# Cross-attention scores in tiles of 32 rows by 64 columns, with a PSUM bank for each row of tiles

## The reference, cut to what matters

```python
q = _ln((x @ Wq + bq).reshape(b, s1, H, HD), qn_w, qn_b)      # 16 heads of 32; 64 queries a batch
k = _ln(kv[..., :HD], kn_w, kn_b)                             # 1585 keys a batch, and 16 more of a second kind
def _attn(q, k, v):
    s = jnp.einsum('bhqd,bhkd->bhqk', q, k) * SCALE
    p = jax.nn.softmax(s, axis=-1)
    return jnp.einsum('bhqk,bhkd->bhqd', p, v)
```

## Time and profile before

| what | before |
|---|---|
| median of 3 runs | 1488.43 us |
| span of the profiled execution | 1487.2 us (1.2 below the median; the page gives no other time of this execution) |
| instructions | 41615 |
| PE busy | 1399.9 us, 94% |
| DVE, ACT, POOL busy | 860.5, 778.8, 500.8 us |
| cross-attention loop | from about 92 to 1182 us |

### The profile page before, as it was taken

The page is one execution under the profiler, slowest core; times in us unless marked ns, Lnnn a source line. Parts: engine busy times, 40 slices in busy tenths (PEclk is TensorE's granted clock), DMA queues, the critical chain, the costliest instruction groups (busy, mean ns, idle before and its releaser), DMA issues. The chain is left out here.

```text
span 1487.2 us, 41615 instructions
## 1 busy us (share of the span) xinstructions
PE 1399.9 (94%) x15754; PEld 1181.9 (79%) x15754; DVE 860.5 (58%) x2005; ACT 778.8 (52%) x1560; POOL 500.8 (34%) x550
## 2 busy tenths in 40 slices
PE   6789999999999999999999999999999899984796
PEld 3378888888888888888888888888878677764696
DVE  7756555655655565556456555655555356655764
ACT  2345555655555565555555555555555433333653
POOL 3333333333333333333333333333323121111455
PEclk9999999999999999999999999999999999995999
DMA  7042110210111121102101101211010100004886
GB/s 253 19 158 77 31 30 16 91 31 16 62 46 30 30 78 30 30 16 92 30 16 62 48 28 30 78 30 31 17 74 2 60 3 30 30 30 178 220 182 140
DMA packets 38937, 91.24 MB, mean 61 GB/s; under 512 B 8135, under 2 KB 11722, under 8 KB 37258
## 3 DMA queue, kind: packets, MB, share of 16 engines
q1 hardware_dynamic: 31904, 72.38, 14.5%
q0 software_dynamic: 6432, 16.32, 4.8%
q10 hardware_dynamic: 434, 0.08, 0.0%
HBM read 71.93 MB, written 36.01 MB: 73 GB/s over the span
## 5 line engine op out<-in xcount | busy, mean ns | idle before, releaser
L1088 POOL TENSOR_TENSOR ksq<-kc 128x512 f32<-128x512 f32 x200 | 208.4, 1042 | 423.8 <-DVE kc L1133 421.9
L1133 DVE TENSOR_TENSOR kc<-psum,bk_sb 128x512 f32<-128x512 f32 x200 | 138.3, 692 | 235.2 <-PE psum L107 234.7
L990 ACT COPY v_sb<-psum 128x512 f32<-128x512 f32 x192 | 112.7, 587 | 277.2 <-PE psum L107 277.2
L1004 ACT ACTIVATE probs<-psum 128x1024 f32<-128x1024 f32 x208 | 201.0, 1023 | 76.6 <-PE psum L1279 76.5
L1081 POOL TENSOR_TENSOR y_lo<-y_sb,y_hi 128x256 fp32r<-128x256 f32 x190 | 139.8, 736 | 231.4 <-ACT y_hi L963 231.3
L1279 PE MATMUL psum<-qbd,k 64*128 64x128 f32 x3328 | 211.9, 278 | 0.1
L1296 PEld LDWEIGHTS psum<-v_sb,probs 128*64 128x64 f32 x6144 | 187.4, 138 | 18.5 <-issue 18.5
L1139 DVE TENSOR_REDUCE kss<-ksq 128x16 f32<-128x512 f32 x200 | 136.5, 682 | 111.4 <-POOL ksq L1088 111.4
L1296 PE MATMUL psum<-v_sb,probs 128*64 128x33 f32 x6144 | 198.1, 224 | 0.0
L1279 PEld LDWEIGHTS psum<-qbd,k 64*128 64x128 f32 x3328 | 193.3, 188 | 4.5 <-ACT k L976 0.3
L107 PE MATMUL psum<-wk_hi,y_hi 128*128 128x512 f32 x400 | 176.8, 442 | 10.7 <-issue 8.6
(11 more groups left out here) (272 smaller groups left out, 1983.9 us busy)
## 6 DMA issues: line engine op xcount, KB each, us to landing
y_sb<-in_y SPq DMA_DIRECT2D x48, 512.0 KB, 3.6
slots_dram<-in_blank SPq DMA_DIRECT2D x9, 2080.0 KB
expert_raw<-in_experts SPq DMA_DIRECT2D x8, 1024.0 KB, 6.9
x_sb<-slots_dram SPq DMA_DIRECT2D x23, 260.0 KB, 3.2
x_sb<-in_x SPq DMA_DIRECT2D x1, 1536.0 KB, 10.7
wq<-in_wq SPq DMA_DIRECT2D x4, 256.0 KB, 4.4
xa_wo<-in_wo SPq DMA_DIRECT2D x1, 1024.0 KB, 12.1
y_tail<-in_y_tail SPq DMA_DIRECT2D x8, 128.0 KB, 21.2
```

Source lines behind the costliest of these rows:

```text
L1004: nc.scalar.activation(probs[:, buf(u), :], psum[:, bank:bank + 2, :].rearrange("p a n -> p (a n)"), ACT.Exp, scale=SCALE).then_inc(s["ex" ...
L1088: nc.gpsimd.tensor_tensor(sq[:, buf(n)], kc[:, buf(n)], kc[:, buf(n)], ALU.mult).then_inc(s["ksq"], 1)
L1133: nc.vector.tensor_tensor(kc[:, buf(n)], psum[:, K_BANK, :], g.bk[:], ALU.add).then_inc(s["kb"], 1)
```

## The change

A chunk's scores are computed by `chunk_scores`: for each of 4 groups of heads, each half of the 128 keys and each of the 4 heads in a group, one matmul whose stationary operand is one head's 64 keys (32 partitions by 64 columns) and whose moving operand is that head's own 64 queries. That is 32 matmuls a chunk. Head row r (32 partitions) writes to bank 3 + r, the two halves of the keys to partitions 0 to 63 and 64 to 127. The columns of a bank are shared: the first chunk of a group has columns 0 to 255, the second 256 to 511. So both chunks lie in the same four banks. The exponential of the first chunk now waits for the scores of the second as well (`u + 1 if j == 0`), the first chunk's scores wait for the exponentials of both chunks before, and the second chunk's no longer wait for an exponential. The exponential reads four pieces of 256 columns. The tail keeps its matmuls (`tail_scores`) and its banks. `place` depends on the unit.

```diff
-                    act.wait_ge(s["sc"], unit(i, u))
+                    act.wait_ge(s["sc"], unit(i, u + 1 if j == 0 else u))
                     act.wait_ge(s["pv"], unit(i, last_unit(u)))
-                    bank = S_PLACES[j]
-                    nc.scalar.activation(probs[:, buf(u), :], psum[:, bank:bank + 2, :].rearrange("p a n -> p (a n)"),
-                                         ACT.Exp, scale=SCALE).then_inc(s["ex"], 1)
+                    if tail(u):
+                        out, scored = probs[:, buf(u), :], psum[:, TAIL_BANK:TAIL_BANK + 2, :].rearrange("p a n -> p (a n)")
+                    else:
+                        out = probs[:, buf(u), :].rearrange("p (r n) -> p r n", r=4)
+                        scored = psum[:, S_BANK:S_BANK + 4, j * GROUPS * SQ:(j + 1) * GROUPS * SQ]
+                    nc.scalar.activation(out, scored, ACT.Exp, scale=SCALE).then_inc(s["ex"], 1)
...
+                def chunk_scores(u, j, guarded):
+                    at_n = [slice(j * GROUPS * SQ + n * SQ, j * GROUPS * SQ + (n + 1) * SQ) for n in range(GROUPS)]
...
+                    for n in range(GROUPS):
+                        for half in range(2):
+                            keys = slice(half * SQ, (half + 1) * SQ)
+                            for r in range(4):
+                                rows, cols = blocks[r]
+                                last = pe.matmul(psum[keys, S_BANK + r, at_n[n]], k32[rows, k_buf(u), n, keys],
+                                                 g.qbd[rows, n, cols], start=not guarded, stop=True, skip_group_check=True)
+                    return last
...
                     pe.wait_ge(s["ke"], projected(i, proj_of(u)))
-                    if j < 2:
-                        pe.wait_ge(s["ex"], unit(i, u - 3 if column(u) < 2 else u - 2))
-                    else:
+                    if j == 0:
+                        pe.wait_ge(s["ex"], unit(i, u - 2 if column(u) == 0 else u - 1))
+                    if j == 2:
                         pe.wait_ge(s["ve"], values_done)
                         pe.wait_ge(s["ke"], turned_done)
...
-        def place(h):
+        def place(h, u):
-            return (h // 2 % 2) * 8 + h // 4 * 2 + h % 2
+            return (h // 2 % 2) * 8 + h // 4 * 2 + h % 2 if tail(u) else h % 4 * GROUPS + h // 4
```

More of the change, by code:

```diff
@@ L747, in cross_attention @@
     K_BANK, V_BANK, TR_BANK, S_BANK, O_BANK = 0, 1, 2, 3, 7
-    S_PLACES = (S_BANK, S_BANK + 2, V_BANK)
+    TAIL_BANK = V_BANK
     with ExitStack() as ctx:
@@ L1266, in scores @@
                         pe.wait_ge(s["kd"], b + 1)
-                    bank = S_PLACES[j]
-                    out = [[psum[:, bank + a, n * P:(n + 1) * P] for a in range(2)] for n in range(GROUPS)]
-                    if guarded:
-                        for n in range(GROUPS):
-                            for a in range(2):
-                                pe.matmul(out[n][a], select[:, {TAIL: 1, UNITS - 1: 2}.get(u, 0), :],
-                                          shift[:, (2 * n + a) * P:(2 * n + a + 1) * P],
-                                          start=(n == 0), stop=False, skip_group_check=True)
-                    for n in range(GROUPS):
-                        for a in range(2):
-                            rows = slice(a * 2 * HD, (a + 1) * 2 * HD)
-                            last = pe.matmul(out[n][a], k32[rows, k_buf(u), n, :], g.qbd[rows, n, :],
-                                             start=not guarded, stop=True, skip_group_check=True)
+                    last = tail_scores(u, guarded) if tail(u) else chunk_scores(u, j, guarded)
                     last.then_inc(s["sc"], 1)
@@ L1296, in weighted @@
                                 last = pe.matmul(psum[j * SQ:(j + 1) * SQ, V_BANK if n else O_BANK, p * VW1:(p + 1) * VW1],
-                                                 probs[:, buf(u), place(h) * SQ:(place(h) + 1) * SQ], v,
+                                                 probs[:, buf(u), place(h, u) * SQ:(place(h, u) + 1) * SQ], v,
                                                  start=(p == 0 and (column(u) == 0 or n == 1)), stop=tail(u), skip_group_check=True)
```

19 lines of the change are left out of this document (added).

## The result

| | before | after |
|---|---|---|
| median, side by side | 1489.03 us (4 runs) | 1499.91 us (4 runs, 1498.15 to 1502.29) |
| ratio to before | | 1.0072, 95% interval 1.0054 to 1.0090 |
| span of the profiled execution | 1487.2 us | 1497.8 us |
| instructions | 41615 | 59867 |

The kernel became slower, by 11 us where 32 were forecast: the direction of the forecast, a third of its size. 1499.91 lies in the range. The profile shows that it comes about otherwise than forecast: the score blocks became 44 us shorter in all, stops took 41 us of that back, and neither was in the sum.

What follows compares the result with a forecast made beforehand. TensorE's own stream was taken as the bound: +22 us for instruction supply, +7 for the wait behind the tail, +3 for changes of form, +32 in sum; 1487.2 + 32 + 1.2 = 1520 us, range 1408 to 1557.

Steps and rivals of the forecast that it cites:

- the prediction's own sign: Forecast wrong if a score block takes under 1.9 us, or the loop grows by more than its blocks and waits.
- What bounds the kernel: Cross-attention loop: TensorE's own stream is the bound, PE busy 1084.9 of 1089.9 us at clock 1.00.
- (1) the array: Score blocks: smaller tiles are a gain for the array; all eight at once give 0.93 us, 1.13 with start and end.
- (2) the supply of instructions: Score blocks: 9 ns an instruction, 32 queued, so 2.22 us a block against 1.99, +22 us over 96 blocks.
- the first rival: Score blocks: all eight tiles run, supply no limit, 1.13 us a block, 1415 us in all; chance 0.20.
- The gap of 30 to 40 ns for four instructions at 1205.76: Self-attention's weighted sum, starting from an empty queue: read as the supply pace, 8 to 10 ns an instruction, 9 taken.
- The rival between: Score blocks: supply of 5 to 7 ns an instruction, 1.3 to 1.8 us a block, 1434 to 1477 us; chance 0.10.
- (3) the shared banks: First exponential waits for both chunks: nothing in two-chunk groups, 0.45 us in 15 tail groups before the values product, 7 us.
- (4) the change of form: Tail keeps 64 by 128 tiles, so 16 blocks change form once more at 0.20 us each: 3 us.
- (5) nothing: Probabilities' order, the exponential's four banks of 256, and the second chunk's dropped wait: no cost or gain.

Runs made afterwards that it cites:

- the wait alone: Kernel before, with only the first exponential of a group also waiting for the second chunk's scores, matmuls and banks as before: 1504.79 us, ratio 1.0095.
- The order with the scores apart: Kernel after, with the second chunk's score matmuls moved behind the next group's first key product: 1518.54 us, ratio 1.0189.
- the mixed tiles: Kernel after, first chunk of a group in tiles of 32 by 64, second in 32 by 128, 192 instructions a block: 1498.49 us, ratio 1.0055.

## Why the prediction was off

The direction was right and the size was not: +11 us (12.6 in the loop) for +32. That the direction came out was luck: the score blocks, which the forecast had at +22 us, became 44 us shorter, and the stops that took this back were not in it. By the prediction's own sign (a block under 1.9 us) its mechanism is wrong.

- **What bounds the kernel:** right. TensorE's stream; 92% busy, and the total follows its blocks and stops.
- **(1) the array** could take all eight tiles: right, eight start within 0.05 us at 699.14, where two did and the next two followed 0.1 us later; the 0.93 us were not reached, because of the next step.
- **(2) the supply of instructions: the step that failed, twice.** It was mis-sized: 9 ns an instruction forecast, 5.3 measured ((1.522 - 0.842) us for 128 instructions), so a block of 1.52 us, not 2.22: -44 us in place of +22. The queue was too small as well: 32 instructions were taken, and the block's quick start has some 64. In 0.1 us in the middle of a block (699.60 to 699.70) 12 loads start, where the forecast had 5 or 6 and the first rival 13. The gap of 30 to 40 ns for four instructions at 1205.76 is not the pace of a long stretch; that it is the start of a stopped queue, as the first rival said, fits, but no run isolates it. The rival between (5 to 7 ns, blocks of 1.3 to 1.8 us) had the block right, and its 1434 to 1477 us would have come about but for the second half of the error: I looked at how fast instructions enter the engine and not at how they reach the core. They come in blocks of 256, usable some 2.8 us after they are asked for, and a score block is 256 instructions in 1.52 us. That cost 41 us, a term that the sum had at nothing. Added up: -44 + 41 instead of +22.
- **(3) the shared banks:** right, in mechanism and size. In groups of two chunks they cost nothing; in the groups with a tail the values product waits for the exponentials, 13 times 0.23 to 0.34 us in the rows, and 7.3 us in all from start to start, for 7 forecast. In the group at 699.14 there is no wait, since a stop ahead of the key product (0.39 us at 702.21) had made PE late anyway. The forecast's own times give 698.5 - 698.1 = 0.4 us a wait and not 0.45, which changes nothing. Part of the agreement is luck: it took a wait for its idle time, and a wait costs the lost overlap of the matmuls around it too (0.73 us for 0.46 with the wait alone), but the waits were shorter than forecast.
- **(4) the change of form:** 0.20 us at the tail, as forecast.
- **(5) nothing:** right; the exponential's mean over 208 is 1.024 us, and was 1.023.
- **The sum by measured terms:** -44 + 3 + 41, together -0.4, for the scores, 7.3 for the wait behind the tail, 1.2 for a stop in a key product, 1.6 for the lower clock behind a stop, 3.2 in the last batch: 12.9, for 12.6 in the loop. Outside it -2.0. The last three terms, 6 us, were not in the forecast either.

Of the two rules cited: TensorEngine Tiling (Array Packing), in the Trainium skill, Instruction Overhead, gives some 60 cycles a matmul. Here a record costs 1.522/128 = 11.9 ns with everything, so that rule is not borne out for many small tiles. TensorE: Matmul & The Clock Gate, in the Trainium skill, Part 3, has about 4 ns from tile to tile. The traces here have 7 ns for the first 33 records of a block and 10.5 on average behind two gaps, each record a load and a multiply.

The order with the scores apart removed the stops and still lost, and so did the mixed tiles in what they gained: the supply of instructions alone doesn't name the bound of such a change. It has three prices here: 10.6 ns a record, 0.16 us or more for each further start and end of a block, and a stop of up to 1.8 us, at times with a lower clock behind it, for a block boundary that is reached too soon.

Open: why a stop lasts 2.0 us on average where the scores are issued twice and 1.0 us in the kernel after (the clock was lower, and two boundaries follow one another); whether ScalarE's lateness (18 us) in the order with scores apart could be taken away; why ScalarE's copy comes later in the last batch; and which stops bring the lower clock. None of these was tried.

## What to carry to other kernels

Before cutting matmuls into smaller tiles, count instructions, not only array time: in this kernel a float32 record of two instructions cost about 10.6 ns on average, and 256 instructions used in less than about 2.8 us could mean a stop. Look at idle time put down to "issue" and at the packets of the instruction queue; the cut worth taking was the one that stayed below both limits (64 by 64, 128 instructions a block, 0.5% faster). Price a new wait by the distance of starts, not by the idle time shown: 0.73 us for 0.46 here. And before a term of a sum is laid to one cause, set the stretches side by side: of the 12 us behind the key products the wait had 7.

## What the runs showed of the hardware

- Instructions come in 16 KB packets of 256; those behind a stop took 0.9 to 1.5 us to move, and PE went on 1.2 to 1.6 us after they had landed (35 of the 36 stops of the kernel after).
- With eight tiles TensorE takes some 64 instructions at 3.5 ns each at the start of a block, and 5.3 ns each from there on average (5.5 ns over 512 in a row); halving the loaded columns or the queries changes a block by 7 to 8% only.
- Behind a stop of about 1 us or more the granted clock can fall to 1.2 GHz, for 3.4 or 6.8 us: so in 56 of 60 falls with the scores issued twice, and once among the 38 stops of the kernel after. Products of 512 columns then start 0.43 us apart and not 0.23.
- Four tiles of 32 rows load 128 columns at once: 1.943 us for 64 records, 30 ns each, where a full-array load takes 112 ns.
- A further start and end of a score block between weighted blocks costs 0.16 us net; the first load of 32 rows behind a full-array product comes 0.32 us later than a full-array load would.
